# Third layer: the products with the values are issued for two steps of keys together

## What is computed

```python
Q = (x @ Wq + bq).reshape(B, S, 16, 16)       # K and V alike
logits = einsum('bqhd,bkhd->bhqk', Q, K) * scale
logits = where(causal, logits, -inf)
attn = softmax(logits, axis=-1)
...                                           # gate: one number for each key, from x
out = einsum('bhqk,bkhd->bqhd', attn * gate[:, None, None, :], V)
return out @ Wo + bo
x = layernorm(x + out)
```

## Time and profile before

| | |
|---|---|
| median of 3 runs | 3404.64 us (3401.59 to 3409.37) |
| the profiled execution: its time, its span | 3401.19 us, 3399.5 us |
| TensorE busy in the span | 3196.4 us, 94% |
| VectorE, ScalarE, GpSimd busy | 55%, 43%, 27% |
| first and last score product (L1601) | 1923.8 and 2684.0 us |

### The profile page before, as it was taken

One profiled execution on the slowest core, in us unless ns is written; L12 is line 12 of the kernel. 1 busy time (PEld: TensorE's weight loads), 2 busy tenths in 40 slices (PEclk: granted clock), 3 DMA queues, 4 the chain that ended last, 5 costly groups with the idle time before them and its releaser, 6 DMA issues. The chain is left out here.

```text
span 3399.5 us, 49734 instructions
## 1 busy us (share of the span) xinstructions
PE 3196.4 (94%) x18258; PEld 2307.8 (68%) x18258; DVE 1874.8 (55%) x3190; ACT 1467.3 (43%) x2700; POOL 906.9 (27%) x819
## 2 busy tenths in 40 slices
PE   7998999999999999999999899999999899999998
PEld 4667657975588755986569546555465588888886
DVE  4557645675466744866454665747667423333332
ACT  3332254423443244423543475554745544444443
POOL 1214324752266412753247101001010011111110
PEclk9999999999999999999999899999999999999999
DMA  5112111011121111111111001010000210000000
GB/s 199 65 41 67 36 28 54 32 44 38 27 72 33 44 23 44 44 46 34 31 51 54 11 2 50 2 27 1 2 26 2 91 62 13 13 13 13 7 7 13
DMA packets 182675, 124.10 MB, mean 37 GB/s; under 512 B 125216, under 2 KB 163360, under 8 KB 178976
## 3 DMA queue, kind: packets, MB, share of 16 engines
q1 hardware_dynamic: 182432, 120.87, 12.6%
HBM read 103.37 MB, written 28.44 MB: 39 GB/s over the span
## 5 line engine op out<-in xcount | busy, mean ns | idle before, releaser
L1673 ACT ACTIVATE l3b_prob<-sums 128x512 f32<-128x512 f32 (+3 forms) x768 | 332.7, 494 | 204.9 <-PE sums L1606 165.8
L1937 PE MATMUL sums<-l_uhi,l_h 128*128 128x512 f32 x1024 | 405.5, 396 | 0.0
L1937 PE MATMUL sums<-l_ulo,l_h 128*128 128x512 f32 x1024 | 405.1, 396 | 0.0
L644 POOL TENSOR_TENSOR l_qrow<-l_vm,l_qst 128x512 fp32r<-128x512 f32 x256 | 352.5, 1389 | 161.8 <-ACT l_qst L638 133.8
L1027 DVE TENSOR_REDUCE l2b_mx<-sums 128x1 fp32r<-128x1024 f32 (+7 forms) x256 | 192.5, 757 | 268.7 <-PE sums L939 267.0
L964 PE MATMUL sums<-sb_nx,l_vx 128*128 128x512 f32 (+3 forms) x768 | 306.7, 509 | 2.1 <-ACT l_od L1002 2.1
L995 ACT ACTIVATE sb_nx<-sums 128x512 f32<-128x512 f32 (+3 forms) x384 | 183.4, 493 | 262.1 <-PE sums L956 256.9
L1601 PE MATMUL sums<-l_qst,l_kst 64*128 64x512 f32 (+3 forms) x768 | 276.7, 425 | 18.6 <-DMA l_qst<-l3b_peak 7.4
L2022 DVE TENSOR_TENSOR l_ulo<-l_made,l_uhi 128x512 fp32r<-128x512 f32 x128 | 90.2, 705 | 363.6 <-ACT l_uhi L1954 363.5
L631 DVE TENSOR_TENSOR l_vm<-l_oT,sums 128x512 f32<-128x512 f32 x256 | 174.3, 682 | 164.5 <-PE sums L623 160.9
L638 ACT CAST l_qst<-l_vm 128x512 fp32r<-128x512 f32 x256 | 158.0, 620 | 242.4 <-DVE l_vm L631 233.3
(11 more groups left out here) (271 smaller groups left out, 8013.5 us busy)
## 6 DMA issues: line engine op xcount, KB each, us to landing
l_ve<-ve SPq DMA_DIRECT2D x32, 512.0 KB, 4.0
l_oe<-oe SPq DMA_DIRECT2D x16, 1024.0 KB, 5.4
between<-sb_x SPq DMA_DIRECT2D x48, 256.0 KB, 2.1
l_vm<-weights_copy SPq DMA_DIRECT2D x32, 352.0 KB, 3.3
sb_nx<-between SPq DMA_DIRECT2D x9, 1024.0 KB, 5.8
weights_copy<-h SPq DMA_DIRECT2D x2, 4096.0 KB, 25.7
l_ve<-inverse SPq DMA_DIRECT2D x32, 256.0 KB, 3.6
l_qst<-l3b_peak SPq DMA_DIRECT2D x512, 0.5 KB, 2.0
```

Of the source, the lines that this page charges most:

```text
L644: pool.tensor_tensor(rlo[:, i % RT, :], routed[:, i % RT, :], rhi[:, i % RT, :].bitcast(F32), ALU.subtract).then_inc(s3.routed_lo, 1)
L1673: act.activation(prob[:, i % RB, j, a, 0:hi - lo], bank(m.ps, part % SCORE, 0, hi - lo), ACT.Exp, scale=SCALE1).then_inc(s.exp_ready, 1)
L1937: run(lambda out, a, x, first, last: pe.matmul(out, a, x, start=first, stop=last))
```

## The change

Step i no longer issues the block of step i - 2. Every odd step from 3 on issues two blocks, those of steps i - 3 and i - 2, and even steps issue none. The last two blocks follow behind the last step as before. Instructions, operands, banks and waits are the same.

```diff
-                    if i >= LAG:
-                        weighted(i - LAG)
+                    if i >= LAG and i % 2:
+                        for ready in (i - LAG - 1, i - LAG):
+                            weighted(ready)
                 for i in range(len(steps) - LAG, len(steps)):
                     weighted(i)
```

## The result

The changed kernel takes 3453.09 us (median of 4 runs, 3452.4 to 3458.04) against 3403.11 (4 runs, 3401.05 to 3409.37) of the kernel before: ratio 1.015, 95% interval 1.0136 to 1.0164. It is slower by 50 us. The sign was forecast, the size was not: 15 us were predicted, and 3453 lies above the stated range of 3386 to 3436.

The account below looks back on a forecast made before the run. TensorE was busy 94% of the span, but chunks 1 to 4 were taken as loaded on TensorE, VectorE and ScalarE. Chunk terms summed to +3.7 us a pass, +15 in four: 3416 profiled, about 3419 predicted; range 3386 to 3436.

Parts of the forecast that it names:

- Effect (b): The wide block between even and odd steps moves behind the odd one, losing its cover under waits for VectorE or ScalarE.
- Keys 1 and 6: Pair of steps in a loaded chunk: maxima still wait for VectorE, then 1.21 us of block stands for 0.35, +0.86.
- Chunk 0: First chunk of each pass: the covered kind of block is missing there, so -0.5 us a pass.
- Keys 0 and 3 of chunk 1: Pair in chunk 1, taken as of the covered kind, with 0.64 us of added block.
- Keys 2 and 5: Pair in a loaded chunk: steps run by ScalarE end near 3.6 us, 1.42 of block follows, +0.1.
- Keys 3 and 4: Pair in a loaded chunk: maxima wait for VectorE as before, 1.64 us of block stands for 0.78, +0.75.
- Keys 3 and 4 of chunk 4: Pair in chunk 4 with narrower tiles that do not wait: put at -0.4 us.
- Chunk 5: Only ScalarE is near: +0.2 us for keys 1 and 6, -0.35 for keys 0 and 7, 0 for the chunk.
- Chunks 6 and 7: Last chunks, with hardly any maxima: -0.2 to -0.4 us a pair, -0.8 a pass.
- The 0.4 that the start of chunk 2 was to give back: Some 0.4 us of chunk 1's loss returns at the start of chunk 2, leaving +1.0 for chunk 1.
- The faster rival: TensorE is the bound everywhere; 92 fixed parts of 0.14 us are saved, 13 to 26 us, about 3386; chance 0.24.
- much slower, by the clock: Longer pauses in odd steps add low-clock stretches, +10 us on the forecast's +15, 3430, up to 3440; chance 0.10.

Follow-up runs that it names:

- late1: The kernel before with double blocks only behind the steps of keys 1 and 6 (or 1 and 2) of chunks 1 to 4: 3419.57 us, ratio 1.0054.
- the short reductions: Kernels before and after, with VectorE's reductions reading only the first 128 columns of each bank of maxima: 3367.35 us (old order) and 3376.28 us (new order).
- light: Double blocks only in chunks 6 and 7, single ones elsewhere as in the kernel before: 3403.54 us, ratio 0.9998.
- b_fill0: The kernel before with 15 useless products a pass in chunk 0's three long waits, order untouched: 3395.61 us, ratio 0.9983.
- a_fill_more: The changed kernel with useless products in steps of keys 6 (chunks 2 to 4), keys 2 (chunk 1) and in chunk 0's long waits: 3433.35 us, ratio 1.0096.
- a_fill: The changed kernel with 48 useless products in waits of keys 6 (chunks 2 to 4) and keys 2 (chunk 1): 3446.58 us, ratio 1.0126.
- mid: The kernel before with each pair's wide block moved into the middle of the odd step, behind its first maxima: 3413.15 us, ratio 1.0032.

## Why the prediction was right, and where it failed

**The cover (right).** Effect (b) is what happens. Keys 1 and 6 were put at +0.86 and went from 4.61 to 5.47; the maxima stayed 0.05 to 0.06 behind a reduction; the doubles take 1.21, 1.43, 1.64 and 1.85 as worked out; chunk 3 is 22.91 for 22.9; `late1` gives the same 5.47 with that block alone moved, and the short reductions take four fifths of the loss away. The pairs of chunks 1 to 7 at full clock sum to +16 us (+20 without the last pair's shift). The forecast's +15 had chunk 0 in it at -0.5 a pass; without it, +17 was forecast. For chunk 0 the filled kernels show +0.73 a pass.

**Terms of that sum.** Some were off and cancelled, so that the closeness of the sum is in part luck. Chunk 0: +0.73 for -0.5. Keys 0 and 3 of chunk 1: -0.44 for +0.64, though this is the pair in which the earlier trace rows show the wait. Keys 2 and 5: +0.28 for +0.1. Keys 3 and 4: +0.54 for +0.75. Keys 3 and 4 of chunk 4: -0.07 for -0.4. Chunk 5, as a stretch beginning with keys 1: 20.40 for 19.9, since the pair of keys 0 and 7 gave nothing for its -0.35 and each of the others lost 0.12 to 0.23. Chunks 6 and 7: about nothing for -0.8, as `light` shows. The 0.4 that the start of chunk 2 was to give back came (0.42). VectorE idled 0.73 behind the double block, not 1.1.

**The faster rival (refuted).** A saved change of layout is worth its 0.14 inside a double (1.21 for 1.35), and nothing of it is to be seen beyond that: with VectorE quick the new order is not shorter at full clock but 0.6 us a pass longer, and in chunks 6 and 7 it gains next to nothing. The price was right, and TensorE was not what everybody waits for.

**The clock (the failed step).** The step that failed is the clock's term. The forecast held it at nothing, and the rival "much slower, by the clock" priced it at "one further stretch like that of chunk 0" a pass, 10 us at half speed of which "the waits cover three quarters", +2.5 us a pass and +10 in all, at a chance of 0.10. Both of its numbers were wrong. A pass has 18 us more at the lower clock, not 10. And the waits cover little: in chunks 1 to 7 the time at the lower clock went from 16.0 to 79.2 us and cost 28 us, 0.45 us for each where 0.25 was taken. With what chunk 0 lost beyond its order's part, some 2.5 by that one instance, it is 31 us for the clock and 19 for the order, together the 50. I had the reason in hand, that "the change makes longer pauses inside odd steps", and saw such pauses only in chunk 0 of the trace before (where the first of them is not even for VectorE but for the transfer of the moved maxima). They came in each of the 12 equal pairs of chunks 2 to 4, and 7 of these ran partly at the lower clock. These 12 pairs hold 9.9 of the 34.4 us; 8.7 more are in chunk 1, and the rest is spread. I also did not carry the clock into the block's price: what stands behind the pause is the double block, 1.21 us at full clock and 2.28 at half. The two losses are not rivals, since both come with the longer wait, and they had to be added in one forecast.

That the clock costs time, and is not only a mark of waits that cost it anyway, is shown by one pair at 5.47 and at 6.76 to 7.20 with the same waits, and by `b_fill0` and `a_fill_more`, which are faster for added work. **Open:** which wait brings the clock down in which pass. The late transfer is the one case in which the trace shows a difference between two passes ahead of the fall. Elsewhere the four passes have the same instructions, and keys 1 and 6 of chunk 3 were wholly at full clock in the first and the fourth and partly low in the second and third (6.76 and 6.83); `a_fill` drove the low stretches out of the filled pairs and found them in others. I can tell what the sum did in each kernel, not forecast a place.

## What to carry to other kernels

A long piece of work that another engine doesn't need belongs under a wait that comes anyway; moved off it, its whole length counts, while what two such pieces save by standing together is worth only what the engine is short of. Price a change of TensorE's order twice, at full clock (compare the shortest instance of each repeated piece) and for the time at the lower clock, since an order may win by the first and lose by the sum, as `mid` did. Where TensorE must wait just ahead of long products, useless products put into the wait can pay for themselves: 60 of them made the kernel before 6.3 us faster. They fill a wait of the length that was planned for: where a transfer came 1.2 us late, the clock fell all the same.

## What was not expected of the hardware

Pauses of TensorE of only 0.4 to 0.8 us, with work between them, stood ahead of a fall to the lower clock (0.39 and 0.78 in chunk 1). In passes of the same instructions in one execution such a fall came or did not. One transfer that landed after 3.2 us instead of 2.0 stood ahead of 13.7 us at the lower clock, and with them the pass took 134.59 us where another took 128.68.
